# A graph network on one core: distances raised in the bank by TensorE, and bank offsets from a table

## The reference

```python
u = -hh[row]
v = hh[col]
coef1 = 1.0 + 2.0 * c0 * duv + c0 * nv
coef2 = 1.0 - c0 * nu
den = 1.0 + 2.0 * c0 * duv + c0 * c0 * nu * nv
ma = (coef1[:, None] * u + coef2[:, None] * v) / den[:, None]
rn = jnp.sqrt(jnp.sum(ma * ma, axis=1))
e = -2.0 / sqrt_c0 * jnp.arctanh(jnp.clip(sqrt_c0 * rn, 1e-08, CLIP))
e_max = jax.ops.segment_max(e, row, num_segments=N)
ex = jnp.exp(e - e_max[row])
denom = jax.ops.segment_sum(ex, row, num_segments=N)
weighted = sqrt_c0 * attention[:, None] * log_h[col]
att_log_h = jax.ops.segment_sum(weighted, row, num_segments=N)
```

## Time and profile before

| | us |
|---|---|
| median of 3 runs | 3235.49 (3232.72 to 6258.4) |
| the profiled execution | 3238.59 |
| its span, first to last instruction | 3236.7 |
| counting loop, first to last item | 139.0 to 635.8 |
| distances | 751 to 1198 |
| DVE busy, whole span | 2362.5 (73%) |
| PE busy, whole span | 1996.3 (62%) |
| ACT busy, whole span | 1830.5 (57%) |

### The profile page before, as it was taken

The page is one execution under the profiler, slowest core; times in us unless marked ns, Lnnn a source line. Parts: engine busy times, 40 slices in busy tenths (PEclk is TensorE's granted clock), DMA queues, the critical chain, the costliest instruction groups (busy, mean ns, idle before and its releaser), DMA issues. The chain is left out here.

```text
span 3236.7 us, 40212 instructions
## 1 busy us (share of the span) xinstructions
PE 1996.3 (62%) x6867; PEld 991.9 (31%) x6868; DVE 2362.5 (73%) x4532; ACT 1830.5 (57%) x2347; POOL 1057.7 (33%) x984
## 2 busy tenths in 40 slices
PE   3477676617777746754884666666666666661546
PEld 1122222213222222211223333333334443430536
DVE  3788888666999967876992777777777777775544
ACT  0155555515777734435882777777778777771010
POOL 1000000000010101101321777777777777773000
PEclk8666766655555559886995777777777777775778
DMA  2133333302555549952551555555555555551616
GB/s 80 37 121 121 121 124 119 136 11 81 202 202 202 206 188 360 372 210 94 211 202 40 155 162 164 163 166 161 171 170 168 164 167 162 164 160 55 232 62 227
DMA packets 288619, 511.07 MB, mean 158 GB/s; under 512 B 39166, under 2 KB 237646, under 8 KB 272518
## 3 DMA queue, kind: packets, MB, share of 16 engines
q1 hardware_dynamic: 254694, 415.04, 36.6%
q0 software_dynamic: 26688, 54.65, 7.1%
q10 hardware_dynamic: 7200, 40.96, 3.3%
HBM read 303.06 MB, written 209.91 MB: 158 GB/s over the span
## 5 line engine op out<-in xcount | busy, mean ns | idle before, releaser
L1767 POOL DMA_INDIRECT es_got<-w,es_idx x808 | 883.2, 1093 | 347.5 <-issue 343.6
L1364 PE MATMUL acc<-src_hot,dst_hot 128*128 128x401 f16 x1008 | 351.7, 468 | 147.2 <-DVE src_hot L1341 96.2
L1902 PE MATMUL en_pv<-en_sq,avg 128*128 128x512 f32 x202 | 199.8, 1091 | 372.4 <-ACT en_sq L2009 372.4
L802 PE MATMUL pd_dn<-hT,pd_lhs 66*128 66x512 f32 (+1 forms) x350 | 282.8, 989 | 104.7 <-DVE pd_m L858 94.5
L1341 DVE TENSOR_SCALAR src_hot<-iota,col_key 128x400 f16<-128x400 f16 x1008 | 321.3, 319 | 0.0
L1339 DVE TENSOR_SCALAR dst_hot<-iota_blk,row_key 128x128 f16<-128x128 f16 x1008 | 253.6, 252 | 81.0 <-PE acc L1364 80.5
L1393 ACT COPY cbuf<-acc 128x401 f32<-128x401 f32 x200 | 98.6, 493 | 225.8 <-PE acc L1364 211.7
L1364 PEld LDWEIGHTS acc<-src_hot,dst_hot 128*128 128x128 f16 x1008 | 102.0, 101 | 396.9 <-issue 392.6
L2037 ACT COPY es_rows<-es_rp 128x512 f32<-128x512 f32 x202 | 118.4, 586 | 172.2 <-PE es_rp L1884 171.0
L1965 DVE TENSOR_TENSOR es_lg<-es_dn,es_w2p 128x512 f32<-128x512 f32 x101 | 69.5, 688 | 199.3 <-PE es_w2p L1858 197.0
L1034 PE MATMUL ns_acc<-ns_w,ns_val 128*65 128x512 f32 (+1 forms) x350 | 158.9, 604 | 68.4 <-DVE ns_w L994 68.4
(11 more groups left out here) (494 smaller groups left out, 4770.9 us busy)
## 6 DMA issues: line engine op xcount, KB each, us to landing
rows<-es_rows SPq DMA_DIRECT2D x202, 256.0 KB, 2.7
counts_part<-cbuf SPq DMA_DIRECT2D x50, 800.0 KB, 3.7
pd_cnt<-counts_part SPq DMA_DIRECT2D x25, 1600.0 KB, 9.4
near<-pd_out SPq DMA_DIRECT2D x25, 1600.0 KB, 6.2
ns_near<-near SPq DMA_DIRECT2D x25, 1600.0 KB, 9.8
ns_cnt<-counts_part SPq DMA_DIRECT2D x25, 1600.0 KB, 6.7
ss_cnt<-counts_part SPq DMA_DIRECT2D x25, 1600.0 KB, 6.6
n_ct<-turned ACTq DMA_DIRECT2D x50, 800.0 KB, 6.1
```

The source lines that it names most:

```text
L802: nc.tensor.matmul(dn[:, i, 0:w], lhs[:, s, :], k["hT"][0:W66, 0, a:a + w], start=True, stop=True).then_inc(prods, 1)
L1364: last = nc.tensor.matmul(acc[:, bass.ds(banks[i], 1), 0:PART + 1], dst_hot[:, s, i, :], src_hot[:, s, i, 0:PART + 1], start=False, stop=F ...
L1767: pool.indirect_dma_start(got[:, s, t, half * 2 * F:(half + 1) * 2 * F], None, d["w23"], bass.IndirectOffsetOnAxis(ap=idx[:, s, half, t:t ...
L1902: nc.tensor.matmul(pv[:, :], avg[:, :], sq[:, :], start=True, stop=True).then_inc(var, 1)
```

## The change

**Counting.** The table of packed words is replaced by two tables: `places`, 1008 integers, each the offset of an item's bank in PSUM, and `newest`, one integer a batch. PE loads `newest`, then eight words of `places` in one load instruction, and uses them as addresses without further arithmetic.

**Distances.** The counts come as `halves` (bf16). DVE compares a block of them with zero (`penalty`), which gives `pen`, 1 where there is no edge. When the products of a block have been clamped out of their banks, PE multiplies `pen` with 1e30 times the identity and adds it to the same banks (`raised`). DVE then lowers the running minimum straight from the banks, on the squared quantity and not on the logarithm. So the banks are free for the next block's products only when they have been lowered. The logarithm goes to `out` without masking. The diagonal's minimum is lowered apart (`own_least`). At the end the 3200 minima are clamped, and ACT and DVE take roots, sum and logarithm of them alone. In near-sums the product with the counts first takes a minimum with 3e38.

```diff
-                then(TS(top[:, :], banki[:, BATCH - 1:NITEM:BATCH], 3, None, ALU.arith_shift_right))
-                then(TS(top[:, :], top[:, :], 3 * BATCH, None, ALU.logical_shift_left))
-                then(TS(banki[:, :], banki[:, :], BATCH - 1, None, ALU.bitwise_and))
-                for i in range(2, BATCH):
-                    then(V.memset(octal[:, i:i + 1], float(8**i)))
-                then(V.tensor_copy(bankf[:, :, :].rearrange("p a b -> p (a b)"), banki[:, :]))
-                then(TT(bankf[:, :, :], bankf[:, :, :], octal[:, :].unsqueeze(1).to_broadcast([1, NBATCH, BATCH]), ALU.mult))
-                then(V.tensor_reduce(word[:, :], bankf[:, :, :], AX.X, ALU.add))
-                then(V.tensor_copy(k["batches"][:, :], word[:, :]))
-                then(TT(k["batches"][:, :], k["batches"][:, :], top[:, :], ALU.bitwise_or))
+                then(TS(k["newest"][:, :], last_w[:, BATCH - 1:NITEM:BATCH], 1.0, None, ALU.add))
+                then(TS(banki[:, :], banki[:, :], 2 * GW - 1, None, ALU.bitwise_and))
+                then(TS(k["places"][:, :], banki[:, :], BANK_BITS, None, ALU.logical_shift_left))
...
                 def load(h, s):
-                    sp.wait_ge(fixed[s], h)
-                    sp.dma_start(cnt[:, s, :], d["counts"][bass.ds((2 * h + s) * P, P), :]).then_inc(loaded[s], 16)
+                    sp.wait_ge(penned[s], h)
+                    sp.dma_start(half[:, s, :], d["halves"][bass.ds((2 * h + s) * P, P), :]).then_inc(loaded[s], 16)
...
+                    pe.wait_ge(penned[s], h + 1)
+                    for i, (a, w) in enumerate(SPANS):
+                        pe.wait_ge(clipped, NS * n + i + 1)
+                        nc.tensor.matmul(dn[:, i, 0:w], far[:, :], pen[:, s, a:a + w],
+                                         start=False, stop=True, skip_group_check=True).then_inc(raised, 1)
...
                 def logarithms(h, s):
-                    b = 2 * h + s
+                    n = 2 * h + s
+                    act.wait_ge(stored[s], 16 * h)
                     for c in range(2):
                         cs = columns(c)
-                        act.wait_ge(added[c], b + 1)
-
-                        nc.scalar.activation(m[:, s, cs], m[:, s, cs], ACT.Ln,
-                                             scale=float(np.exp(-HALF_OFF))).then_inc(logs[c], 1)
+                        act.wait_ge(added[c], n + 1)
+                        nc.scalar.activation(out[:, s, cs], m[:, s, cs], ACT.Ln).then_inc(logs[c], 1)
...
+                act.wait_ge(top_near, 1)
+                nc.scalar.activation(topc[:, 1, :], topc[:, 0, :], ACT.Sqrt, bias=1.0).then_inc(top_rooted, 1)
+                act.wait_ge(top_rooted, 1)
+                nc.scalar.sqrt(topc[:, 0, :], topc[:, 0, :]).then_inc(top_rooted, 1)
+                act.wait_ge(top_near, 2)
+                nc.scalar.activation(topc[:, 0, :], topc[:, 1, :], ACT.Ln).then_inc(top_rooted, 1)
...
+                def own(h, s):
+
+                    n = 2 * h + s
+                    here = bass.ds(n * P, P)
+                    for c in range(2):
+                        dve.wait_ge(logs[c], n + 1)
+                    V.tensor_tensor(out[:, s, here], out[:, s, here], off[:, :], ALU.mult).then_inc(diag_off, 1)
+                    dve.wait_ge(diag_off, n + 1)
+                    V.tensor_tensor(out[:, s, here], out[:, s, here], self_near[:, :], ALU.add).then_inc(fixed[s], 1)
+
+                def penalty(h, s):
+
+                    n = 2 * h + s
                     dve.wait_ge(loaded[s], 16 * h + 16)
-                    nc.vector.scalar_tensor_tensor(out=out[:, s, cs], in0=cnt[:, s, cs], scalar=1.0, in1=m[:, s, cs],
-                                                   op0=ALU.min, op1=ALU.mult).then_inc(masked_[c], 1)
-
-                def own(h, s):
-
-                    b = 2 * h + s
-                    here = bass.ds(b * P, P)
-                    for c in range(2):
-                        dve.wait_ge(masked_[c], b + 1)
-                    V = nc.vector
-                    V.scalar_tensor_tensor(out=dcnt[:, :], in0=cnt[:, s, here], scalar=1.0, in1=self_near[:, :],
-                                           op0=ALU.min, op1=ALU.mult).then_inc(diag_fixed, 1)
-                    V.tensor_tensor(out[:, s, here], out[:, s, here], off[:, :], ALU.mult).then_inc(diag_fixed, 1)
-                    dve.wait_ge(diag_fixed, 2 * b + 2)
-                    V.tensor_tensor(out[:, s, here], out[:, s, here], dcnt[:, :], ALU.add).then_inc(fixed[s], 1)
+                    if not (isinstance(n, int) and n < 2):
+                        dve.wait_ge(raised, NS * (n - 1))
+                    V.tensor_scalar(pen[:, s, :], half[:, s, :], 0.0, None, ALU.is_equal).then_inc(penned[s], 1)
+                    dve.wait_ge(penned[s], h + 1)
+                    V.scalar_tensor_tensor(out=own_least[:, s, :], in0=pen[:, s, bass.ds(n * P, P)], scalar=BIG,
+                                           in1=self_least[:, :], op0=ALU.mult, op1=ALU.add).then_inc(leasted[s], 1)
 
                 def lower(h, s):
-                    dve.wait_ge(fixed[s], h + 1)
-                    for c in range(2):
-                        cs = columns(c)
-                        nc.vector.tensor_tensor(top[:, cs], top[:, cs], out[:, s, cs], ALU.min).then_inc(lowered[c], 1)
-                    for c in range(2):
-                        dve.wait_ge(lowered[c], 2 * h + s + 1)
-
-                nc.vector.tensor_scalar(off[:, :], k["ident"][:, :], -1.0, 1.0, ALU.mult, ALU.add).then_inc(not_diag, 1)
-                nc.vector.tensor_scalar(self_near[:, :], k["ident"][:, :], SELF_NEAR - HALF_OFF, None,
-                                        ALU.mult).then_inc(not_diag, 1)
-                nc.vector.memset(topc[:, 0:1], 0.0).then_inc(used, NSLOT)
-                nc.vector.memset(top[:, :], 0.0).then_inc(top_zero, 1)
-                dve.wait_ge(top_zero, 1)
-                dve.wait_ge(not_diag, 2)
-                for s in range(2):
-                    for c in range(2):
-                        clipped(0, s, c)
+                    n = 2 * h + s
+                    dve.wait_ge(topped, n)
+                    for i, (a, w) in enumerate(SPANS):
+                        dve.wait_ge(raised, NS * n + i + 1)
+                        V.tensor_tensor(top[:, a:a + w], top[:, a:a + w], dn[:, i, 0:w], ALU.min).then_inc(lowered, 1)
+                    dve.wait_ge(leasted[s], h + 1)
+                    dve.wait_ge(lowered, NS * n + 2 * NS)
+                    here = bass.ds(n * P, P)
+                    V.tensor_tensor(top[:, here], top[:, here], own_least[:, s, :], ALU.min).then_inc(topped, 1)
...
+                def step(h, s, first=False, last=False):
+
+                    n = 2 * h + s
+                    clip(h, s, 0)
+                    if not (first and n < 2):
+                        own(h - 1, s)
+                    if not (first and n < 1):
+                        joined(h + s - 1, 1 - s, 0)
+                    clip(h, s, 1)
+                    if not (first and n < 1):
+                        joined(h + s - 1, 1 - s, 1)
+                    lower(h, s)
+                    if not last:
+                        penalty(h + s, 1 - s)
+                penalty(0, 0)
+                step(0, 0, first=True)
+                step(0, 1, first=True)
+                with dve.Fori(0, NBK // 2 - 1) as h:
+                    step(h + 1, 0)
+                    step(h + 1, 1)
...
-                    nc.vector.tensor_tensor(w_[:, s, cs], z[:, s, cs], cnt[:, s, cs],
-                                            ALU.mult).then_inc(weighed[s][c], 1)
+                    nc.vector.scalar_tensor_tensor(out=w_[:, s, cs], in0=z[:, s, cs], scalar=3e38, in1=cnt[:, s, cs],
+                                                   op0=ALU.min, op1=ALU.mult).then_inc(weighed[s][c], 1)
...
-                        word = pe.value_load(k["batches"][0:1, bass.ds(b, 1)], min_val=0, max_val=2**31 - 1)
-                        banks = [(word >> 3 * i & 7).with_bounds(min_val=0, max_val=7) for i in range(BATCH)]
-                        newest = ((word >> 3 * BATCH << 3) + banks[BATCH - 1]).with_bounds(min_val=0, max_val=NW - 1)
-                        pe.wait_ge(cleared, newest + 1)
+                        newest = pe.value_load(k["newest"][0:1, bass.ds(b, 1)], min_val=1, max_val=NW)
+                        _, places = nc.values_load_multi_w_load_instructions(
+                            k["places"][0:1, bass.ds(BATCH * b, BATCH)], engines=(mybir.EngineType.PE,),
+                            min_val=0, max_val=7 * BANK,
+                            skip_runtime_bounds_check_because="written as BANK times (window & 7)")
+                        pe.wait_ge(cleared, newest)
                         for i in range(BATCH):
                             if i % 4 == 0:
                                 pe.wait_ge(hot, BATCH * b + i + 4)
```

(2 more changed lines are left out.)

132 lines of the change are left out of this document (69 added, 63 removed).

## The result

The changed kernel takes 3099.8 us (median; 3096.5 to 3103.8), the kernel before 3239.7 us beside it: ratio 0.9576, 95% interval 0.9548 to 0.9603. 3102 us had been predicted. One of the four executions of the kernel before took 6258.4 us; the ratio leaves it out. The profiled execution's span is 3094.6 us, before 3236.7.

The account below looks back on a forecast made before the run. The prediction took PE's sequencer as the counting loop's bound and DVE as the distance stage's. From 3238.6 us, counting -82, tables -4 and distances -50 gave 3102.6, stated as 3102, with a range of 3080 to 3330.

Parts of the forecast that it names:

- T: Counting loop: time of the eight-word load on PE's sequencer, taken at its lower bound, 0.56 us, with little confidence.
- the upper bound: Counting loop: every loaded word a trip of its own, 0.20 us each, the load 1.7 us, 6.5 under DMA; +105 us.
- rival (1): Counting loop: words loaded one by one; 3290 us at 0.20 a word, 3371 at 0.30; chances 0.25 (3170 to 3300), 0.20 beyond.
- PE's batch: Counting loop: PE's sequencer needs 2.40 us a batch plus the eight-word load, 2.96 in all, where 3.94 was measured before.
- The 3.29 of DVE: Counting loop: DVE's 3.17 us sets the pace, 3.29 a batch with some coupling over a ring of three; -82 us.
- Tables: Ahead of counting: 5.66 us of DVE rows become 1.7; -4 us.
- Distances: Distance stage: steps from 16.04 to 14.0 to 14.1 us, 22 steps -43, the end -8.5; together -50 us.
- rival (3): Load cheap, clock rises under fuller PE: distances lose 0.4 of waiting, counting at 3.2; 3083 us; chance 0.43 together with the forecast.
- The tail's parts: End of distances: 11.2 us from last clamp to first reduction, 4.6 behind it; -8.5 us.

Follow-up runs that it names:

- the moved load: Changed kernel with three kinds of load; this one takes eight words from a table moved by one word, 4 bytes past a multiple of 16; kernel 3174.5 us.
- the ring of six: Changed kernel with six buffers for the one-hot tiles in place of three, nothing else: 3089.4 us, ratio 0.9531.
- the padded kernel: Changed kernel with newest window and eight places in one nine-word load, each row padded to twelve words: 3071.9 us, ratio 0.9468.
- the distances alone: Kernel before with only the new distances and near-sums, counting still by the packed word: 3177.8 us, ratio 0.9792.
- counts twice: Changed kernel with each group of counts written to memory a second time, for more DMA traffic: 3135.5 us, ratio 0.9657.
- rows of nine: Changed kernel with newest window and eight places in one nine-word load, rows not padded: 3214.3 us, ratio 0.9895.

## Why the prediction was right, and where it wasn't

**What bounds.** Right. PE's sequencer set the counting loop's pace, though the rows put the wait down to DVE: taking its register operations away gave 79 us, putting sixteen a batch back took more than that.

**The load, T.** The term that was wrong, though the sum survived it. I took T as 0.56 (0.30 for the row, 0.06 behind it, 0.20 for traffic) by the argument that a load is one instruction that "is slow to start and then streams". It doesn't stream: in most loads tried here each word costs 0.235 us, near the 0.20 of the upper bound, and of those rival (1) was true. This load escaped it because it asks for eight words from a multiple of 16 bytes, which go four at a time: its row is 0.59 quiet and 0.94 on the mean with DMA, so T is 1.00 with the same 0.06 behind it. That T came out on the low side was luck: the argument that chose it was wrong.

The Trainium skill, in Runtime: NRT & Kernel Launch, Instruction fetch mechanics, gives about 200 ns per register "even for bulk". The loads whose words go one by one are near it, with 0.235 from a tile in SBUF; the loads from an aligned start go against it, with eight words in 0.59.

Had the table begun one word further on, T would have been near the moved load's mean of 3.06. By the prediction's own sum that is a batch of 5.5 and a kernel of some 3375 us, an estimate: rival (1)'s time at 0.30 a word. The chance of 0.45 that I gave it was not too much; nothing in the trace of before could tell.

**PE's batch.** Predicted 2.40 + T = 2.96. With T at 1.00 it would be 3.40; measured, by the ring of six, 3.25. So the count of register operations was right within 0.15, and T was off by more. PE, at 3.25, and not DVE, at 3.17, is then the slower one. The size of T did cost time: the padded kernel, whose PE batch is shorter, ran the loop in 17 us less.

**The 3.29 of DVE.** Measured 3.288, but that agreement is luck. I had put the 0.12 over DVE's own 3.17 down to single late loads with PE otherwise at 2.96. The runs show PE at 3.25, nearly level with DVE. The padded kernel, with one load less, runs at 3.167.

**Tables.** -4 predicted, -5.8 seen, but the first one-hot matrix starts between 129.2 and 135.3 us in the kernels with the new tables, and at 135.1 and 137.6 in the two with the old ones: the term can't be told within some microseconds.

**Distances.** -50 predicted, -58.7 measured. By their rows: lowering 3.86 (3.8), comparison 0.99 (1.0), raising 2.87 (2.7), step 13.81 (14.0 to 14.1). The last 22 steps gave 49 us where 43 were forecast. Of these 6 us some 2 go with the clock: the sum held PE at 1.2 GHz for every block (11 us of products), and 8 of 25 blocks ran at 2.4 GHz in 5.64. Where all blocks of this trace had 1.2 GHz a step took 13.99; where every second one had 2.4 GHz it took 13.83. Some 2 more are the last step (11.90), and the rest is a step at 1.2 GHz of 13.99 for the 14.09 of the sum. The clock's part is the half of rival (3) which the sum left out; its other half, counting at 3.2 a batch, didn't come. The tail's parts were off both ways. From the last clamps to the first reduction it takes 1025.64 - 1011.67 = 14.0, not 11.2:

```profile
1009.60 2.07 DVE L873 TENSOR_SCALAR pd_m<-pd_dn 128x512 f32<-128x512 f32 x4
...
1019.30 0.29 DVE L886 TENSOR_TENSOR pd_out<-pd_out,pd_off 128x128 f32<-128x128 f32 x1 [1.64 <-ACT pd_out L844]
...
1025.11 0.29 DVE L886 TENSOR_TENSOR pd_out<-pd_out,pd_off 128x128 f32<-128x128 f32 x1 [1.73 <-ACT pd_out L844]
...
1025.64 0.48 DVE L949 TENSOR_REDUCE pd_topc<-pd_dn 128x1 f32<-128x128 f32 x2
```

DVE stands in its own order behind the diagonals of the last two blocks, which wait for ACT's logarithms, while the running minimum has been ready since 1017.7. Behind the reductions it took 2.3, not 4.6, since a table load of ACT ran under them: 16.3 together, against 15.8. The kernel before took 24.9 from its last clamps to its first reduction, so the tail gave 8.6 us, and 8.5 were forecast.

**What stays open.** Why the steps differ between kernels with the same code in this stage. Counting the blocks from 0, the fast blocks of the changed kernel are even ones (6, 8 and so on), and the steps around them alternate between 14.29 and 13.38. In the distances alone and in the padded kernel the fast blocks are odd ones (from 5 and from 1 on), and the steps are 13.68 and 13.69 throughout. The distance stage is 388.4 us in the first, 385.5 and 379.3 in the others; it is 387 to 389 in the two other kernels whose fast blocks are even (counts twice, rows of nine), and 379 to 382 in the five others whose fast blocks are odd from 1 on. So up to 9 us of a kernel's time go with which blocks get the faster clock; that this is the cause is not shown. What decides that was not tried, nor what the step would be without the raising on PE.

## What to carry to other kernels

Count the sequencer's register operations of an engine that issues short work; at 0.09 to 0.10 us each, two of them outweigh the 0.17 us from one matmul to the next, and a table of ready-made numbers pays. Start every multi-word register load on a multiple of 16 bytes, and pad its rows to four words: the same words then cost a third (0.59 for 1.94) to two fifths (0.85 for 2.17). Before an operation is moved, look which queue's store waits for its result, and what is queued behind that store.

## What the runs showed that I hadn't expected

A register load's cost depends on where it starts: eight words 0.59 us from a multiple of 16 bytes, 1.94 from 4 bytes further, and under DMA traffic up to 1.94 and 4.33. TensorE's granted clock went from 2.4 to 1.2 GHz and back from one block to the next, for stretches of the distance stage; in the rows above the fast block of products came after 0.28 us of idle time, the slow one after 1.88. The idle time alone doesn't tell the level: the slow blocks from 889 to 945 us came after 0.28, too. And a load of one word, whose row says 0.30 quiet and 0.35 on the mean, costs the sequencer 0.50: eight of them made a batch of 6.28 us where PE needs 3.25 with one load of eight (mean 0.94), so (3.03 + 0.94) / 8.
